# One V product for two groups of heads in an attention and expert kernel on one core

## Chip, cores and metric

The kernel runs on one core of one Trainium2 chip. The metric is the device time of one execution in microseconds; the median of the runs shown is 392.6 us.

## What is computed

For 2048 rows of 256 (8 batches of 256 rows), the reference adds two parts to x:

```
q = layernorm(x); kv = context; seg_id = itok
kv_c = kv @ W_kvc; q_c = q @ W_dq
q_nope, q_rope = q_c @ W_uq, rope(q_c @ W_qr)       # 16 heads
k_nope, k_rope, v from kv_c
scores = (q_nope.k_nope + q_rope.k_rope) * scale, masked to k in [seg_id - 8, seg_id]
x = x + (softmax(scores) @ v) @ W_o
gates: the best two of 8 experts for layernorm(x)
x = x + mean of relu(layernorm(x) @ expert_w + expert_b) over the two
```

No seg_id of the input is above 127, so only the first 128 context rows of each batch matter; a flag worked out from the input picks the path described here.

## The kernel before

Rows are worked in 16 tiles of 128 (two a batch). The weights of the up-projections are folded into the query and output weights first, so that a head works in the 64 latent columns of the context: a head's V is the same 128x64 matrix `v_cur` for all heads of a batch, and its output weight is 64x256. The 16 heads of a tile are four groups of four, so there are 64 groups. `walk` runs slots: slot i = 8 b + k starts group i and carries on the groups before it. Each engine has its own `slot` function, and the order of the calls in it is the order of the engine's queue; counting semaphores are the only link between engines. Slots up to 15 are written out, 16 to 55 are a loop over batches, the last 8 and 6 more to drain are written out again. g is k modulo 4, t the tile, r is k modulo 2 and picks a buffer.

In slot i TensorE has, in this order (its `slot`): the gate products of tile t-2 where g is 1; four transposes of the queries of group i (L1092); the query product of group i+1 in three passes of 512 columns (`mm3`, L674 to L676), with rope parts and unrotated parts in one bank `B_Q`; the transposes of the probabilities of group i-2 (L1119); the scores of group i (L1135), four heads in float32, each recorded as two matmuls; where g is 0 the transposes of a normalised row tile (L1144), where g is 2 the two small rank products (L1155, L1156); the output products of group i-3; in slots 2 to 8 the latent product (L371) and in slots 1 to 7 the transposes of x (L354) for later batches; the V product of group i-2 (L1205).

The output of a group is two blocks of 128 rows (two heads of 64 each). For groups below `PLAIN` the output product is one float32 matmul per block with `oT` and `wo_all` (L1182); for the others it is three passes, high by high, high by low and low by high (`mm3`, L674 to L676, with `oT_hi`, `oT_lo`, `wo_hi`, `wo_lo`), accumulated in `B_Y` over the four groups of a tile. The V product is two matmuls, one for the even and one for the odd heads of the group. Each has the 64 columns of `v_cur` stationary and 256 columns of `pT` moving, and writes one half of the partitions of bank `B_O`; the two stand on different halves of the array.

ScalarE in slot i copies the transposed queries qT of group i (L1273), does the second pair of heads' exponentials of group i-1 (`exps`, L1230), copies pT of group i-2 (L1280), copies the unrotated query parts of group i+1 (L1292), does the first two exponentials of group i, in early slots casts expert weights (`we_high`, L387), copies V's result out of `B_O` as `oT` or `oT_hi` (L1320), and in slots 12 to 15 casts output weights (`wo_high`, L312).

VectorE in slot i has small steps of the gate (`top_two`), then the low half `oT_lo` of group i-3 (L1572: `B_O` less `oT_hi`), the two rope products of group i+1 (L1587, L1588), the reciprocal of the sums of group i-1 (L1596), the masked scores and maxima of group i (L1625), and at g = 2 the sum x2 of the last tile (L1634) with its statistics, at g = 3 the places of rows and the normalised row (L1682 to L1701).

GpSimd joins the rope parts to the query (L1349, group i+1), normalises the probabilities (L1363, group i-1), takes the root of the second norm (L1369), scatters normalised rows to HBM (L1382), builds masks, and in slots 12 to 15 makes the low halves of the output weights (`wo_low`, L316).

After slot 63 the experts' jobs begin (turn, product and store of 128 gathered rows each), eleven of them between the draining slots, the rest after them, and then the sums are stored.

The fold of the output weights (`fold_o`, L301) has the form of the V product: per pair of heads two matmuls of 64 stationary and 256 moving columns on the two halves of the array; a call has four matmuls for two pairs.

Of the kernel before, what the change touches and what calls it, by code (L numbers as in the profile page):

```python
# [23 lines left out]
F32 = mybir.dt.float32  # L24
F32R = mybir.dt.float32r
# [40 lines left out]
def kernel_program(nc, x, ctx_t, ctx_near, itok, w_kvc, w_dq, w_uq_t, w_qr, w_uk_t, w_kr, w_uv_t, w_o,  # L66
                   gate_w, gate_b, expert_w, expert_b, rope, w_kvc_t, out):
    with ExitStack() as ctx:
# [148 lines left out]
        prec = [sb(f"prec{i}", [P, HG]) for i in range(2)]  # L217
        pT = [sb(f"pT{i}", [P, HG, P]) for i in range(2)]
        oT_hi = [sb(f"oT_hi{i}", [P, 2, P], F32R) for i in range(2)]
        plain_mem = ExitStack()  # L220
        oT = [plain_mem.enter_context(nc.sbuf_tensor(f"oT{i}", [P, 2, P], F32)) for i in range(2)]
        plain_mem.close()
        oT_lo = [sb(f"oT_lo{i}", [P, 2, P], F32R) for i in range(2)]
        m_after, m_before = sb("m_after", [P, P]), sb("m_before", [P, P])
# [170 lines left out]
        FOLDS, EXPERT_PIECES = PAIRS // 2, DC * NE // 2  # L395
        PLAIN = 13

        def plain(n):

            return isinstance(n, int) and n < PLAIN  # L400

        def piece_of(i, count):
# [584 lines left out]
        def _(pe):  # L987
# [60 lines left out]
            def dense(f):  # L1048

                kc, j = f % GPT, dense_turned(f // GPT)  # L1050
                if f == 0:
                    pe.wait_ge(m["oT_lo_done"], GROUPS - PLAIN)
                elif f == 1:
                    pe.wait_ge(m["x2_done"], TILES)
                else:
                    pe.wait_ge(m["relu_done"], f - 1)
                cols = slice(512 * kc, 512 * kc + 512)
                z = DENSE_BANK[f % 2]
                pe.matmul(z, ones2[:], bias2[:, cols], start=True, stop=False)
                for c in range(DC):  # L1060
                    mm = mm3(pe, z, xT_hi[j][:, c, :], xT_lo[j][:, c, :], we_hi[:, c, cols], we_lo[:, c, cols],
                             start=False, stop=(c == DC - 1))
                mm.then_inc(m["e_done"], 1)
# [10 lines left out]
            def slot(b, k):  # L1074
# [90 lines left out]
                if isinstance(i, int) and i == 2:  # L1165
                    fold_o(pe, 3)
                if live(i - 3, GROUPS):

                    gp = (k - 3) % GPT
                    at_least(pe, "oT_done", i - 2)  # L1170
                    if not plain(i - 3):
                        pe.wait_ge(m["oT_lo_done"], i - 2 - PLAIN)
                    if isinstance(i, int) and i - 3 < FOLDS:
                        pe.wait_ge(m["wo_done"], FOLDS)
                    if not isinstance(i, int):
                        pe.wait_ge(m["wo_lo_done"], FOLDS)
                    if gp == 0:
                        at_least(pe, "x2_done", TPB * b + (k - 3) // GPT)
                    for q in range(2):
                        first, last = gp == 0 and q == 0, gp == GPT - 1 and q == 1  # L1180
                        if plain(i - 3):
                            mm = pe.matmul(B_Y[:, 0:D], oT[1 - r][:, q, :], wo_all[:, 2 * gp + q, :],  # L1182
                                           start=first, stop=last)
                        else:
                            mm = mm3(pe, B_Y[:, 0:D], oT_hi[1 - r][:, q, :], oT_lo[1 - r][:, q, :], wo_hi[:, 2 * gp + q, :],
                                     wo_lo[:, 2 * gp + q, :], start=first, stop=last)
                    mm.then_inc(m["y_done"], 1)
# [4 lines left out]
                if piece_of(i - 1, B - 1):  # L1192
                    x_turn(pe, i)
                if live(i - 2, GROUPS):

                    if (k - 2) % SLOTS == 0:
                        at_least(pe, "v_ready", b + (k - 2) // SLOTS + 1)
                    at_least(pe, "pT_sb", i - 1)
                    at_least(pe, "oT_done", i - 2)
                    if not plain(i - 3):  # L1200
                        pe.wait_ge(m["oT_lo_done"], i - 2 - PLAIN)
                    if isinstance(i, int) and i == 2:
                        pe.wait_ge(m["wo_done"], 2)
                    for odd in range(2):
                        mm = pe.matmul(B_O[KVC * odd:KVC * odd + KVC, 0:D], v_cur[:], pT[r][:, odd::2, :],  # L1205
                                       start=True, stop=True)
                    mm.then_inc(m["pv_done"], 1)
# [17 lines left out]
        def _(act):  # L1225
# [41 lines left out]
            def slot(b, k):  # L1267
# [9 lines left out]
                if live(i - 2, GROUPS):  # L1277
                    at_least(act, "pT_done", i - 1)
                    at_least(act, "pv_done", i - 3)
                    act.copy(pT[r][:], B_PT[:, :].rearrange("p (h n) -> p h n", h=HG)).then_inc(m["pT_sb"], 1)  # L1280
                late_turn = isinstance(i, int) and i >= GROUPS
# [32 lines left out]
                if piece_of(i - 7, EXPERT_PIECES):  # L1314
                    we_high(act, i - 7)
                if live(i - 2, GROUPS):
                    at_least(act, "pv_done", i - 1)
                    at_least(act, "y_done", i - 3)
                    cols = oT[r][:] if plain(i - 2) else oT_hi[r][:]
                    act.copy(cols, B_O[:, 0:D].rearrange("p (q n) -> p q n", q=2)).then_inc(m["oT_done"], 1)  # L1320
                if piece_of(i - 12, FOLDS) and i < 2 * SLOTS:
# [108 lines left out]
        def _(dve):  # L1430
# [128 lines left out]
            def slot(b, k):  # L1559
# [7 lines left out]
                if g == 1 and live(t - 2, TILES) and not late:  # L1567
                    top_two("gate_step", t - 2, [1])
                if live(i - 3, GROUPS) and not plain(i - 3):
                    at_least(dve, "oT_done", i - 2)  # L1570
                    at_least(dve, "y_done", i - 4)
                    dve.tensor_tensor(oT_lo[1 - r][:], B_O[:, 0:D].rearrange("p (q n) -> p q n", q=2),  # L1572
                                      oT_hi[1 - r][:].bitcast(F32), ALU.subtract).then_inc(m["oT_lo_done"], 1)
                if isinstance(i, int) and i == 8:
                    dve.wait_ge(S("ld_gate_bias"), 16)
                    dve.wait_ge(S("counted"), 6)
                if live(i + 1, GROUPS):

                    j1 = ((k + 1) // GPT) % 2
                    if isinstance(i, int) and i == -1:  # L1580
# [8 lines left out]
                                      a.rearrange("p h (a n) -> p h a n", a=2)[:, :, ::-1, :], sin,  # L1589
                                      ALU.mult).then_inc(m["rope_parts"], 1)  # L1590
                if piece_of(i - 1, B - 1):
                    x_norm(dve, i)
# [4 lines left out]
                if (k - 2) % SLOTS == 0 and live(bv, B):  # L1597

                    at_least(dve, "pv_done", SLOTS * bv)
                    if isinstance(bv, int) and bv == 0:  # L1600
                        dve.wait_ge(S("kcat_done"), 4)
                    kv = kcat[:, bass.ds(bv, 1), 0:KVC]
                    dve.tensor_copy(v_cur[:], kv.rearrange("p a n -> p (a n)")).then_inc(m["v_ready"], 1)
# [27 lines left out]
                if g == 2 and live(t - 1, TILES):  # L1631

                    at_least(dve, "y_done", GPT * t)
                    dve.tensor_tensor(x2_of(t - 1), B_Y[:, 0:D], x2_of(t - 1), ALU.add).then_inc(m["x2_done"], 1)  # L1634
# [169 lines left out]
```

## Time and profile before

| what | value |
| --- | --- |
| median of 3 runs | 392.6 us (391.34 to 395.19) |
| the profiled execution | 392.47 us |
| its span, first to last instruction | 390.6 us |
| mean granted TensorE clock | 0.979 |
| busy: TensorE matmul, weight load | 353.8 us (91%), 290.2 us (74%) |
| busy: VectorE, ScalarE, GpSimd | 276.5 (71%), 262.5 (67%), 234.0 us (60%) |
| chain that ended last: TensorE, VectorE, issue, GpSimd | 73%, 9%, 7%, 5% |

The profile is of one execution. Times in rows are from the span's start. PE is TensorE, PEld its weight loads, DVE VectorE, ACT ScalarE, POOL GpSimd. Matmuls are pipelined: a row's duration overlaps with the next, so that the cost of a piece on TensorE is read from one start to the next.

### The profile page before, as it was taken

Reading aid. Unit: us, or ns where it says so; the run is one execution under the profiler, and the core shown is the slowest. Engines: PE = TensorE matmul, PEld = TensorE weight load, DVE = VectorE, ACT = ScalarE, POOL = GpSimd, SP = SyncE. Lnnn points to the kernel's source line nnn. Section 1 sums busy time; section 2 is a strip of 40 time slices with the busy share of each in tenths; the row PEclk is TensorE's granted clock in tenths of the full one; section 3 lists DMA queues with packets and bytes.
Section 4 is the critical chain, followed back from the end, with each engine's and each line's share of the span. In section 5 each row is a group of like instructions: output and inputs, shape, how many; then the busy total and the mean of one; then the engine's idle time right before and its main releaser. Section 6 shows DMA issues by size and latency. Waiting matters only on the chain.

```text
span 390.6 us, 10358 instructions
## 1 busy us (share of the span) xinstructions
PE 353.8 (91%) x2507; PEld 290.2 (74%) x2507; DVE 276.5 (71%) x1395; ACT 262.5 (67%) x907; POOL 234.0 (60%) x326
## 2 busy tenths in 40 slices
PE   0979999999999999999999999999999788999940
PEld 0866777776778887888888888888887677888730
DVE  2358789687887878778777777778779566444365
ACT  1327777788877887877878877878788544555430
POOL 4626456367987767768577675776865355455500
PEclk9989999999999999999999999999999999999985
DMA  8955040000000000000000000000000354453178
GB/s 273 345 198 215 3 110 3 1 3 27 2 30 1 30 10 17 27 0 27 0 27 27 0 27 0 27 27 0 30 2 28 97 166 127 146 141 113 34 262 294
DMA packets 15094, 28.27 MB, mean 72 GB/s; under 512 B 2892, under 2 KB 10719, under 8 KB 14416
## 3 DMA queue, kind: packets, MB, share of 16 engines
q1 hardware_dynamic: 11408, 20.25, 16.3%
q0 software_dynamic: 2960, 6.94, 5.0%
q10 hardware_dynamic: 688, 0.64, 0.6%
q8 instruction: 16, 0.26, 0.3%
q14 instruction: 22, 0.18, 0.2%
HBM read 17.81 MB, written 10.91 MB: 74 GB/s over the span
## 4 chain that ended last, share of the span: by engine, by line
PE 73%; DVE 9%; issue 7%; POOL 5%; DMA 2%; ACT 2%; ACTq 0%; DVEq 0%; POOLq 0%
PE psum L1135 12%; PE psum L674 9%; PE psum L675 9%; PE psum L676 9%; PE psum L1205 8%; PE psum L1092 8%; PE psum L1119 6%; DVE x_all L1557 2%; DMA wcat<-in_w_kvc 2%; PE psum L1182 2%; PE psum L371 2%; POOL prob L1363 2%; PE psum L1014 1%; POOL q_sb L1349 1%; PE psum L1026 1%
## 5 line engine op out<-in xcount | busy, mean ns | idle before, releaser
L1230 ACT ACTIVATE prob<-nsc,nmax 128x128 f32<-128x128 f32 x256 | 100.7, 396 | 42.9 <-DVE nmax L1625 42.8
L1349 POOL TENSOR_TENSOR q_sb<-rope_a,rope_b 128x256 f32<-128x256 f32 x64 | 47.6, 743 | 57.6 <-DVE rope_b L1588 53.5
L1625 DVE CUSTOM_DVE_ANT_0 nsc<-psum,mask 128x128 f32<-128x128 f32 x256 | 58.9, 286 | 21.3 <-PE psum L1135 21.3
L1363 POOL TENSOR_TENSOR prob<-prob,prec 128x512 f32<-128x512 f32 x64 | 67.1, 1049 | 7.3 <-DVE prec L1596 7.3
L1135 PE MATMUL psum<-kT_all,qT 128*128 (+1 forms) x512 | 69.0, 278 | 1.1 <-ACT qT L1273 1.1
L1135 PEld LDWEIGHTS psum<-kT_all,qT 128*128 128x128 f32 x512 | 62.9, 193 | 2.4 <-ACT qT L1273 2.0
L1417 POOL DMA_INDIRECT halves<-jout,jidx x33 | 32.2, 977 | 30.2 <-ACT jout L1245 13.4
L1230 ACT ACTIVATION_READ_ACCUMULATOR prob<-nsc,nmax 128x1 f32 x256 | 48.4, 189 | 0.0
L1092 PE MATMUL psum<-ident,q_sb 128*128 128x128 f32 x256 | 42.4, 289 | 1.8 <-POOL q_sb L1349 1.7
L1092 PEld LDWEIGHTS psum<-ident,q_sb 128*128 128x128 f32 x256 | 27.2, 142 | 20.9 <-issue 12.3
L1205 PE MATMUL psum<-pT,v_cur 128*64 128x256 f32 x256 | 41.7, 405 | 0.0
L1273 ACT COPY qT<-psum 128x512 f32<-128x512 f32 x64 | 37.5, 585 | 5.4 <-PE psum L1092 3.2
L1119 PE MATMUL psum<-ident,prob 128*128 128x128 f32 x256 | 38.6, 272 | 0.4 <-POOL prob L1363 0.4
L1119 PEld LDWEIGHTS psum<-ident,prob 128*128 128x128 f32 x256 | 31.6, 140 | 9.6 <-POOL prob L1363 0.9
L1382 POOL DMA_INDIRECT slots<-row,place_i x26 | 26.9, 1036 | 16.2 <-POOL row L1377 11.2
L1280 ACT COPY pT<-psum 128x512 f32<-128x512 f32 x64 | 36.5, 571 | 0.1
L674 PE MATMUL psum<-wo_hi,oT_hi 128*128 128x256 f32 x102 | 32.9, 322 | 2.2 <-issue 1.2
L1587 DVE TENSOR_TENSOR rope_a<-psum,ropeq 128x256 f32<-128x256 f32 x64 | 26.7, 416 | 7.7 <-PE psum L676 7.6
L674 PE MATMUL psum<-wq_hi,qc_hi 96*128 96x512 f32 x64 | 30.7, 480 | 0.0
L1292 ACT COPY q_sb<-psum 128x256 f32<-128x256 f32 x64 | 24.2, 377 | 6.9 <-DVE rope_b L1588 6.8
L675 PE MATMUL psum<-wo_lo,oT_hi 128*128 128x256 f32 x102 | 28.5, 279 | 0.0
L676 PE MATMUL psum<-wo_hi,oT_lo 128*128 128x256 f32 x102 | 28.3, 278 | 0.0
(204 smaller groups left out, 864.7 us busy)
## 6 DMA issues: line engine op xcount, KB each, us to landing
wanted<-slots SPq DMA_DIRECT2D x33, 129.0 KB, 2.4
wo_raw<-in_w_o SPq DMA_DIRECT2D x2, 1024.0 KB, 15.5
we_raw<-in_expert_w SPq DMA_DIRECT2D x1, 2048.0 KB, 9.0
half<-halves SPq DMA_DIRECT2D x4, 512.0 KB, 7.3
x_all<-in_x SPq DMA_DIRECT2D x2, 640.0 KB, 17.9
slots<-pad_row SPq DMA_DIRECT2D x8, 129.0 KB, 3.4
we_raw<-in_ctx_near SPq DMA_DIRECT2D x1, 1024.0 KB, 12.0
out<-x_all SPq DMA_DIRECT2D x2, 512.0 KB, 4.7
```

Of the source, the lines that this page charges most:

```text
L674: pe.matmul(out_ap, l_hi, r_hi, start=start, stop=False)
L675: pe.matmul(out_ap, l_hi, r_lo, start=False, stop=False)
L676: return pe.matmul(out_ap, l_lo, r_hi, start=False, stop=stop)
L1092: mm = pe.transpose(B_QT[:, P * h:P * h + P], q_sb[r][:, h, :], ident[:])
L1119: mm = pe.transpose(B_PT[:, P * h:P * h + P], prob[r][:, h, :], ident[:])
L1135: mm = pe.matmul(B_S[r][:, h, :], qT[r][:, h, :], batch_keys, start=True, stop=True)
L1205: mm = pe.matmul(B_O[KVC * odd:KVC * odd + KVC, 0:D], v_cur[:], pT[r][:, odd::2, :], start=True, stop=True)
L1230: e = act.activation(prob[r][:, h, :], nsc[r][:, h, :], ACT.Exp, bias=nmax[r][:, h:h + 1], scale=-1.0, accum_out=psum_h[r][:, h:h + 1])
L1273: act.copy(qT[r][:], B_QT[:, :].rearrange("p (h n) -> p h n", h=HG)).then_inc(m["qT_sb"], 1)
L1349: pool.tensor_tensor(q_sb[1 - r][:, :, KVC:P], rope_a[1 - r][:], rope_b[1 - r][:], ALU.add).then_inc(m["rope_joined"], 1)
L1363: pool.tensor_tensor(p[:], p[:], prec[1 - r][:, :].unsqueeze(2).to_broadcast([P, HG, P]), ALU.mult).then_inc(m["prob_normed"], 1)
L1625: e = dve.tensor_tensor_reduce(nsc[r][:, h, :], B_S[r][:, h, :], mask[(k // GPT) % 2][:], -SCALE, BIG, ALU.add, ALU.min, nmax[r][:, h:h + 1])
```

## The change

The V product is made in odd slots alone, for the two groups before, with 512 moving columns in each half; the output products of both groups are made in the next (even) slot. `pT`, `oT`, `oT_hi` and `oT_lo` hold two groups and are single buffers. ScalarE copies the whole bank `B_O` once, at the end of the odd slot; VectorE makes the low half of all of it once, in the even slot, and there behind the rope products instead of ahead of them. `PLAIN` goes from 13 to 12. Counts on `pv_done`, `y_done`, `oT_done` and `oT_lo_done` are pairs instead of groups.

```diff
-        pT = [sb(f"pT{i}", [P, HG, P]) for i in range(2)]
-        oT_hi = [sb(f"oT_hi{i}", [P, 2, P], F32R) for i in range(2)]
+        pT = sb("pT", [P, 2 * HG, P])
+        oT_hi = sb("oT_hi", [P, 4, P], F32R)
...
-        PLAIN = 13
+        PLAIN = 12
...
+        def pair_of(b, k):
+
+            return (SLOTS // 2) * b + k // 2
...
-                if live(i - 3, GROUPS):
-
-                    gp = (k - 3) % GPT
-                    at_least(pe, "oT_done", i - 2)
-                    if not plain(i - 3):
-                        pe.wait_ge(m["oT_lo_done"], i - 2 - PLAIN)
...
+                if k % 2 == 0 and live(i - 4, GROUPS):
+
+                    gp, p = (k - 4) % GPT, pair_of(b, k - 4)
+                    at_least(pe, "oT_done", p + 1)
+                    if not plain(i - 4):
+                        pe.wait_ge(m["oT_lo_done"], p + 1 - PLAIN // 2)
...
-                    for q in range(2):
-                        first, last = gp == 0 and q == 0, gp == GPT - 1 and q == 1
...
+                    for q in range(4):
+                        first, last = gp == 0 and q == 0, gp == GPT - 2 and q == 3
...
-                if live(i - 2, GROUPS):
-
-                    if (k - 2) % SLOTS == 0:
-                        at_least(pe, "v_ready", b + (k - 2) // SLOTS + 1)
+                if k % 2 == 1 and live(i - 3, GROUPS):
+
+                    p = pair_of(b, k - 3)
+                    if (k - 3) % SLOTS == 0:
+                        at_least(pe, "v_ready", b + (k - 3) // SLOTS + 1)
                     at_least(pe, "pT_sb", i - 1)
-                    at_least(pe, "oT_done", i - 2)
+                    at_least(pe, "oT_done", p)
...
                     for odd in range(2):
-                        mm = pe.matmul(B_O[KVC * odd:KVC * odd + KVC, 0:D], v_cur[:], pT[r][:, odd::2, :],
-                                       start=True, stop=True)
+                        mm = pe.matmul(B_O[KVC * odd:KVC * odd + KVC, :], v_cur[:], pT[:, odd::2, :], start=True, stop=True)
...
-                    at_least(act, "pv_done", i - 3)
-                    act.copy(pT[r][:], B_PT[:, :].rearrange("p (h n) -> p h n", h=HG)).then_inc(m["pT_sb"], 1)
+                    at_least(act, "pv_done", pair_of(b, k - 2))
+                    act.copy(pT[:, HG * r:HG * r + HG, :], B_PT[:, :].rearrange("p (h n) -> p h n", h=HG)).then_inc(m["pT_sb"], 1)
...
-                if live(i - 2, GROUPS):
-                    at_least(act, "pv_done", i - 1)
-                    at_least(act, "y_done", i - 3)
-                    cols = oT[r][:] if plain(i - 2) else oT_hi[r][:]
-                    act.copy(cols, B_O[:, 0:D].rearrange("p (q n) -> p q n", q=2)).then_inc(m["oT_done"], 1)
+                if k % 2 == 1 and live(i - 3, GROUPS):
+                    p = pair_of(b, k - 3)
+                    at_least(act, "pv_done", p + 1)
+                    at_least(act, "y_done", p)
+                    cols = oT[:] if plain(i - 3) else oT_hi[:]
+                    act.copy(cols, B_O.rearrange("p (q n) -> p q n", q=4)).then_inc(m["oT_done"], 1)
...
-                if live(i - 3, GROUPS) and not plain(i - 3):
-                    at_least(dve, "oT_done", i - 2)
-                    at_least(dve, "y_done", i - 4)
-                    dve.tensor_tensor(oT_lo[1 - r][:], B_O[:, 0:D].rearrange("p (q n) -> p q n", q=2),
-                                      oT_hi[1 - r][:].bitcast(F32), ALU.subtract).then_inc(m["oT_lo_done"], 1)
...
                                       a.rearrange("p h (a n) -> p h a n", a=2)[:, :, ::-1, :], sin,
                                       ALU.mult).then_inc(m["rope_parts"], 1)
+                if k % 2 == 0 and live(i - 4, GROUPS) and not plain(i - 4):
+                    p = pair_of(b, k - 4)
+                    at_least(dve, "oT_done", p + 1)
+                    at_least(dve, "y_done", p)
+                    dve.tensor_tensor(oT_lo[:], B_O.rearrange("p (q n) -> p q n", q=4), oT_hi[:].bitcast(F32),
+                                      ALU.subtract).then_inc(m["oT_lo_done"], 1)
```

## Rows read from the trace of the kernel before

**Rows 1.** Busy time by stretch, columns PE, PEld, DVE, ACT, POOL, clock, DMA, GB/s.

```profile
240.00:280.00 40.00, 40.00 (x306) 33.19 (x304) 31.31 (x182) 31.90 (x120) 28.63 (x39) 1.00 0.06 20
```

**Rows 2.** The chain that ended last, slots 53 and 54: start, us, what.

```profile
262.60 0.58 PE psum L1205 x4
263.18 0.59 PE psum L1092 x4
```

**Rows 3.** Timeline of TensorE, slots 53, 54 and 56: start, us, operation.

```profile
260.83 1.06 PE L1135 MATMUL psum<-kT_all,qT 128*128 x8
261.65 0.37 PE L674 MATMUL psum<-wo_hi,oT_hi 128*128 128x256 f32 x1
261.85 0.28 PE L675 MATMUL psum<-wo_lo,oT_hi 128*128 128x256 f32 x1
...
262.53 0.65 PE L1205 MATMUL psum<-pT,v_cur 128*64 128x256 f32 x4
263.11 0.66 PE L1092 MATMUL psum<-ident,q_sb 128*128 128x128 f32 x4
...
264.73 1.06 PE L1135 MATMUL psum<-kT_all,qT 128*128 x8
...
265.68 0.36 PE L674 MATMUL psum<-wo_hi,oT_hi 128*128 128x256 f32 x1
...
273.70 0.36 PE L674 MATMUL psum<-wo_hi,oT_hi 128*128 128x256 f32 x1
```

**Rows 4.** Timeline of ScalarE, slots 53 and 54.

```profile
261.23 0.56 ACT L1280 COPY pT<-psum 128x512 f32<-128x512 f32 x1
...
262.66 0.40 ACT L1230 ACTIVATE prob<-nsc,nmax 128x128 f32<-128x128 f32 x1 [0.60 <-DVE nmax L1625]
...
263.45 0.35 ACT L1320 CAST oT_hi<-psum 128x256 fp32r<-128x256 f32 x1
263.80 0.59 ACT L1273 COPY qT<-psum 128x512 f32<-128x512 f32 x1
```

**Rows 5.** Timeline of VectorE, slots 53, 54 and 56.

```profile
262.12 0.29 DVE L1625 CUSTOM_DVE_ANT_0 nsc<-psum,mask 128x128 f32<-128x128 f32 x1 [0.58 <-PE psum L1135]
...
264.23 0.42 DVE L1572 TENSOR_TENSOR oT_lo<-psum,oT_hi 128x256 fp32r<-128x256 f32 x1
264.58 0.41 DVE L1587 TENSOR_TENSOR rope_a<-psum,ropeq 128x256 f32<-128x256 f32 x1
264.91 0.41 DVE L1588 TENSOR_TENSOR rope_b<-psum,ropeq 128x256 f32<-128x256 f32 x1
...
272.28 0.41 DVE L1572 TENSOR_TENSOR oT_lo<-psum,oT_hi 128x256 fp32r<-128x256 f32 x1
```

**Rows 6.** Timeline of GpSimd, slot 53.

```profile
262.19 0.75 POOL L1349 TENSOR_TENSOR q_sb<-rope_a,rope_b 128x256 f32<-128x256 f32 x1
```

**Rows 7.** Groups by line, whole span: form, count, busy us, mean ns, idle before.

```profile
L1273 ACT COPY qT<-psum 128x512 f32<-128x512 f32 x64 | 37.5, 585 | 5.4 <-PE psum L1092 3.2
...
L392 DVE TENSOR_TENSOR we_lo<-we_raw,we_hi 128x512 fp32r<-128x512 f32 x8 | 7.0, 878 | 0.0
...
L421 DVE TENSOR_TENSOR wq_lo<-psum,wq_hi 96x512 fp32r<-96x512 f32 x2 | 1.4, 678 | 0.0
```

**Rows 8.** The chain that ended last, slot 2, a fold of output weights.

```profile
38.05 1.01 PE psum L301 x8
```

**Rows 9.** Timeline of ScalarE and TensorE, slots 5, 9 and 10.

```profile
54.19 0.38 ACT L1292 COPY q_sb<-psum 128x256 f32<-128x256 f32 x1
...
78.05 0.61 ACT L387 CAST we_hi<-we_raw 128x512 fp32r<-128x512 f32 x1
...
79.51 1.11 PE L1135 MATMUL psum<-kT_all,qT 128*128 128x128 f32 x8
```

**Rows 10.** Timeline of TensorE and VectorE near 321 us.

```profile
321.89 0.44 PE L1144 MATMUL psum<-ident,row 128*128 128x128 f32 x2 [0.99 <-DVE row L1701]
...
321.36 0.47 DVE L1701 TENSOR_SCALAR row<-x_all,mv,rstd 128x256 f32<-128x256 f32 x1 [1.75 <-POOL rstd L1369]
```

## What I predict before seeing the changed kernel

> **What bounds the kernel now.** I read the busy time by stretch first. From 240 to 280 us TensorE is busy for every microsecond, at the full clock, while VectorE and ScalarE stand near 80% and GpSimd near 70% [rows 1]. Then the chain of waits: through the slots it is TensorE alone, products end to end [rows 2]. The starts on TensorE's timeline give one slot its prices [rows 3]: from the transposes of the queries (L1092, 263.11) to the scores (L1135, 264.73) 1.62; scores to the output product (L674, 260.83 to 261.65) 0.82; output products to the V product (261.65 to 262.53) 0.88, of which the first takes 0.20, the other five about 0.117 each (0.585), and the rest, 0.09, is a gap ahead of V; V to the next transposes (262.53 to 263.11) 0.58. Sum 3.90. A slot with the rank products costs 0.13 more (264.73 to 265.68 is 0.95 against 0.82); what the other kinds of slot add is the same before and after.
>
> But TensorE is not alone at the limit. ScalarE's timeline [rows 4] has, after the scores: exponentials at 262.66, the output copy at 263.45, the query copy (qT) at 263.80 to 264.39, and the next scores at 264.73. ScalarE waited 0.60 before the exponentials and almost nowhere after: the loop scores, maxima, exponentials, output copy, query copy, next scores has about 0.3 us of slack.
>
> **The change part by part.** Slots now alternate. An odd slot has no output products and one V product over both groups; an even slot has twelve output products and no V.
>
> V, on TensorE. Two products cost 2 x (0.09 + 0.58) = 1.34 a pair of slots. The new one, 512 columns a half, is not in the trace. Lower bound: nothing more for the doubled columns, 0.58. Upper: the halves no longer run beside each other, two of today's for each half, about 1.7. The nearest row is the folding of the weights (L301), the same form with two halves of 64 columns and twice 256 columns in a row: 1.01 for eight records [rows 8]. I take 1.01, with 0.09 ahead of it: a gain of 0.24 a pair. Output products: two first ones at 0.20 become one, a gain of 0.08. Together 0.32 of TensorE's time a pair.
> The trace shows the cost of the switch between V's half-width form and full-width work: transposes after V hold the chain for 0.59 [rows 2]. The Trainium skill (TensorEngine Tiling (Array Packing), Key Properties) says that a change of tiling mode drains TensorE; by that rule half the drains go, and the sum would be the full 0.32 a pair, which is the first rival below.
>
> The path through ScalarE in an odd slot. I lay the odd slot on the times of rows 3 to 5. Scores start 260.83; the first maximum runs at 262.12 and the exponentials at 262.66 [rows 4, 5], as before: nothing in between changes. The output copy starts at 263.45; V, now at 261.65 + 0.09, has ended by 263, so it does not hold it (the copy of pT ends at 261.79 [rows 4] and may hold V's start by 0.1, under this cover). The copy is now 128x512 instead of 128x256: the nearest rows are the query copy, 128x512 from PSUM, 585 ns [rows 7], against 350 ns. Successive operations overlap by about 0.10, so the query copy starts at 263.45 + 0.48 = 263.93 and ends at 264.52; with 0.05 for the wait the even slot's scores start at 264.57. TensorE by itself would be there at 260.83 + 0.82 + 0.09 + 1.01 + 1.62 = 264.37. So it stands 0.20, and, since the weights of the first score product are no longer loaded under other work, about 0.08 more. Of the 0.32, 0.28 is gone. In the even slot ScalarE has no output copy and is early; its time cannot be given back there, since TensorE sets that slot.
> The Trainium skill (TensorEngine Tiling (Array Packing), PSUM Bottleneck) warns that faster tiled products do not speed up the emptying of PSUM, which may become the bound; the trace agrees so far as its ScalarE loop has only 0.3 us of slack.
>
> VectorE in the even slot. The low half (L1572) is now 128x512 and stands behind the two rope products. At 256 columns it took 0.42 [rows 5]; at 512 the nearest rows are 678 ns (L421, 96x512 from PSUM) and, as the upper end, 878 ns (L392) [rows 7]; the lower end is the old 0.42. I take 0.69. In the slot of the rank products the ropes move from 264.58 to 264.23, the low half starts two steps of 0.33 later, 264.89, and ends at 265.58, 265.63 with the wait. TensorE wants it at 264.57 + 0.82 + 0.08 + 0.13 = 265.60. In the other even slot VectorE comes free at 272.28 [rows 5]: 272.28 + 0.66 + 0.69 + 0.05 = 273.68, against TensorE, whose first output product stood at 273.70 [rows 3] and by the same steps comes 0.08 earlier, 273.62. So the low half costs 0.03 to 0.07 a pair. What waits behind it on VectorE is the reciprocal and the maxima; GpSimd's normalisation of the odd group then starts about 0.3 later, which is in time for its transposes a slot later. The rope joins (L1349) come 0.3 earlier except behind the scatter issues, where GpSimd starts the join at 262.19 and ends it at 262.94 whatever VectorE does [rows 6]: 0.2 after TensorE's new 262.75, hidden under the stand of 0.20 above.
> Sum for the 24 pairs of slots 16 to 63: 0.32 - 0.28 - 0.06 is about -0.02 a pair, a loss of 0.5 us in all, which is nothing within its error.
>
> The slots before 16. Pairs 3 to 8 carry the latent product, which waits for the copy of the unrotated queries (L1292, to 54.57 [rows 9]). Odd slots reach it at 54.30 instead of a product later: a stand of 0.3. The odd slot then ends at 57.10 (before 57.15), and the even one, with 0.87 more of plain output products and without V and its gap (0.67), takes 0.20 more: 0.17 a pair lost, 0.5 in three. In pairs 9 to 12 ScalarE also casts expert weights (L387, 78.05, step 0.51) between the exponentials and the output copy [rows 9]: copy at 78.56, query copy 79.05 to 79.63, scores at 79.68 instead of 79.51, and 0.20 + 0.08 in the even slot: 0.45 a pair, 0.9 in two. Slots 13 to 16 wait for GpSimd's low halves of the output weights, before and after: 0. Group 12 becoming split (PLAIN 12) falls there too: 0.
>
> The end. The last pair's V now comes whole in slot 65. The copy behind it is 0.22 longer, the low half 0.27, the products 0.70: 1.19 more on the way to the last tile's sum. TensorE does about 0.37 less in slot 65 and is there earlier: 0.8 net. That way is on the path: TensorE stood 0.99 us for that row (L1144 at 321.89), and VectorE 1.75 for its root [rows 10].
>
> The single buffers of pT and oT cost nothing: the slots between their uses are filled by the work above, and the halved counts change no order on a DMA queue.
>
> Sum: 0.5 + 0.5 + 0.9 + 0.8 = 2.7 us (the loop, pairs 3 to 8, pairs 9 to 12, the end). The profiled execution took 392.47 (span 390.6, 1.9 around it, unchanged): 395.2. The median of the runs shown is 392.6, so the profile stands for them.
>
> **The rivals.** First, TensorE stays the bound: 0.32 x 24 = 7.7 us gained, less 0.8 at the end: 385.6. For it: TensorE is the whole chain of waits. Against it: the ScalarE loop in rows 4, unless the wide copy takes nearer 0.35 than 0.585. Second, slower: VectorE's low half decides. At 0.88 instead of 0.69 every even slot stands 0.19 longer: 24 x 0.19 = 4.6 us, 399.8. It decides once the low half takes more than about 0.66, at the place where TensorE waits ahead of the twelve products. For it: VectorE runs without a pause from the maxima to that point. Against it: L421 is the nearer row, as it reads PSUM. Third, the change doesn't do what it says: V's halves of 512 columns run one behind the other, 0.7 more per odd slot; 0.5 of that shows after the stand of 0.20: 12 us, 407. The L301 row speaks against it. Fourth, the stand is half what I find: 24 x 0.14 = 3.4 us better, 391.8.
>
> **How the numbers follow.** The forecast, 395.2 with its own range from 392 to 398, gets 0.5; TensorE-bound 0.15; the half stand 0.15; VectorE's low half 0.17; V's halves apart 0.03. About 1% (3.9 us) is what a measurement of this kernel tells from no change: faster is below 388.7, slower above 396.5. Faster: 0.15, and 0.02 of the half stand's lower edge, 0.17. Slower: 0.17 + 0.03 + 0.13 of the forecast's upper part, 0.33. The rest, 0.50, is within 1%. The range for 8 in 10 goes from 387.5 to 400: it leaves out most of the first rival and the third.
>
> **What would show it.** Right: TensorE idle 0.1 to 0.3 before the scores of even slots, released by the query copy; that copy starting 0.48 after an output copy of 0.58; the low half ending within 0.1 of the first output product; V at about 1.0 from its start to the transposes; pairs of slots near the 7.93 (3.90 and 4.03) that they take now. Wrong: pairs of 7.6 (first rival), output products waiting over 0.2 for the low half (second), V near 1.7 (third).

## The result, and the profile after

The changed kernel takes 400.78 us (median of 4 runs, 399.68 to 401.42) against 393.36 (391.34 to 395.19) for the kernel before, run beside it: 1.0187 times as long [1.0127, 1.0247]. I had said 395.2, at most 400. The profiled execution took 401.42 (span 399.7). The starts of the query transposes divide the 9.1 us between the spans: slot 17 starts 1.07 later than before (110.84 and 111.91), slot 61 5.78 (292.04 and 297.82), slot 63 6.77 (300.54 and 307.31), and from there to the end it is 92.35 instead of 90.07.

Of the first 1.07, 0.40 stands already at slot 1 (29.17 and 29.57), ahead of all that the change moves (the kernel of b4_turns_late, which is the kernel before up to slot 63, is there at 28.55); slot 2, where V no longer stands, is 0.69 shorter (6.65 and 5.96), which I had not priced; from slot 3 to slot 17 the loss is 1.36 (69.79 and 71.15), where I had 1.4. The end lost 2.28 instead of 0.8, and the slots from 17 to 62 lost 5.7 instead of 0.5: slots 17 to 60 4.71, of which the pairs with g = 1 and 2 have 0.97 and those with g = 3 and 0 3.74, and slots 61 and 62 0.99.

The share of the chain of waits by engine, from the profile's page, shows what kind of loss it is. TensorE had 73%, and has 55% now:

```profile
PE 55%; DVE 16%; issue 12%; POOL 7%; ACT 5%; DMA 2%; DVEq 1%; ACTq 0%; SPq 0%; POOLq 0%
```

First the parts that I had priced. The chain in slots 53 and 54 (start, us, what) has V at 1.01 for both groups, as in [rows 8], with the transposes at 0.59 behind it, as in [rows 2]:

```profile
267.05 1.01 PE psum L1209 x4
268.05 0.59 PE psum L1096 x4
```

ScalarE's timeline in the same slots, beside [rows 4]: the wide output copy takes 0.56, and the query copy starts 0.47 behind its start (I had 0.48):

```profile
268.60 0.56 ACT L1324 CAST oT_hi<-psum 128x512 fp32r<-128x512 f32 x1
269.07 0.58 ACT L1276 COPY qT<-psum 128x512 f32<-128x512 f32 x1
```

TensorE's timeline, slots 54 (g = 2) and 56 (g = 0), beside [rows 3]:

```profile
267.99 0.66 PE L1096 MATMUL psum<-ident,q_sb 128*128 128x128 f32 x4
268.40 0.48 PE L678 MATMUL psum<-wq_hi,qc_hi 96*128 96x512 f32 x1
...
268.95 0.39 PE L680 MATMUL psum<-wq_hi,qc_lo 96*128 96x512 f32 x1
...
269.78 1.15 PE L1139 MATMUL psum<-kT_all,qT 128*128 x8
...
270.88 0.39 PE L678 MATMUL psum<-wo_hi,oT_hi 128*128 128x256 f32 x1
...
272.40 0.60 PE L1096 MATMUL psum<-ident,q_sb 128*128 128x128 f32 x4
272.75 0.47 PE L678 MATMUL psum<-wq_hi,qc_hi 96*128 96x512 f32 x1
...
275.96 0.66 PE L1096 MATMUL psum<-ident,q_sb 128*128 128x128 f32 x4
...
277.68 1.16 PE L1139 MATMUL psum<-kT_all,qT 128*128 128x128 f32 x8
278.67 0.38 PE L1148 MATMUL psum<-ident,row 128*128 128x128 f32 x2
279.32 0.36 PE L678 MATMUL psum<-wo_hi,oT_hi 128*128 128x256 f32 x1 [0.27 <-issue]
```

and before, the starts of slots 55 and 56 and the scores of slot 56:

```profile
267.14 0.66 PE L1092 MATMUL psum<-ident,q_sb 128*128 128x128 f32 x4
...
271.04 0.66 PE L1092 MATMUL psum<-ident,q_sb 128*128 128x128 f32 x4
...
272.67 1.06 PE L1135 MATMUL psum<-kT_all,qT 128*128 128x128 f32 x8
```

In slot 54 the scores come 1.79 behind the transposes instead of 1.62 (I had 0.20 to 0.28 more) and the slot takes 4.41. With the odd slot's 3.62 the pair takes 8.03; I had about 7.95, before it was 7.93. That pair is nearly right. The pair with g = 3 and 0 is not: 3.56 and 5.23 instead of 3.90 and 4.58. In slot 56 the first output product comes 1.64 behind the scores; before it was 273.70 - 272.67 = 1.03, and I had 0.06 more.

VectorE's timeline says why, after:

```profile
269.47 0.42 DVE L1586 TENSOR_TENSOR rope_a<-psum,ropeq 128x256 f32<-128x256 f32 x1
...
270.14 0.68 DVE L1594 TENSOR_TENSOR oT_lo<-psum,oT_hi 128x512 fp32r<-128x512 f32 x1
...
272.71 0.42 DVE L1639 TENSOR_TENSOR x_all<-psum,x_all 128x256 f32 x1 [0.62 <-PE psum L680]
...
274.29 0.42 DVE L1586 TENSOR_TENSOR rope_a<-psum,ropeq 128x256 f32<-128x256 f32 x1
...
277.52 0.44 DVE L1706 TENSOR_SCALAR row<-x_all,mv,rstd 128x256 f32 x1 [0.37 <-POOL rstd L1373]
277.89 0.41 DVE L1586 TENSOR_TENSOR rope_a<-psum,ropeq 128x256 f32<-128x256 f32 x1
...
278.55 0.67 DVE L1594 TENSOR_TENSOR oT_lo<-psum,oT_hi 128x512 fp32r<-128x512 f32 x1
```

and before, in the same slots (the low half and the ropes of slot 56 are in [rows 5]):

```profile
266.86 0.42 DVE L1634 TENSOR_TENSOR x_all<-psum,x_all 128x256 f32 x1
...
268.68 0.42 DVE L1587 TENSOR_TENSOR rope_a<-psum,ropeq 128x256 f32<-128x256 f32 x1
```

Read each against the start of its slot. The sum x2 of the last tile ran 0.28 ahead of slot 55 (which began at 267.14), without a wait. Now it runs 0.31 behind the start (272.40), and has waited 0.62 for the output products. Before, V stood between those products and the next slot, and the sum had that time; now the twelve products are the last work of the slot. Its statistics follow on VectorE, and the ropes of slot 55 start 1.89 behind its start instead of 1.54. From there it goes through GpSimd, whose queue has the rope join, the normalisation and only then the root. GpSimd after and before:

```profile
275.13 0.73 POOL L1353 TENSOR_TENSOR q_sb<-rope_a,rope_b 128x256 f32<-128x256 f32 x1 [2.27 <-DVE rope_b L1587]
275.82 1.04 POOL L1367 TENSOR_TENSOR prob<-prob,prec 128x512 f32<-128x512 f32 x1
276.81 0.57 POOL L1373 TENSOR_TENSOR rstd<-veps,half_neg 128x1 f32<-128x1 f32 x1
```

```profile
269.51 0.73 POOL L1349 TENSOR_TENSOR q_sb<-rope_a,rope_b 128x256 f32<-128x256 f32 x1 [1.56 <-DVE rope_b L1588]
270.20 1.04 POOL L1363 TENSOR_TENSOR prob<-prob,prec 128x512 f32<-128x512 f32 x1
271.20 0.57 POOL L1369 TENSOR_TENSOR rstd<-veps,half_neg 128x1 f32<-128x1 f32 x1
```

The root starts 0.85 into slot 56 instead of 0.16. VectorE waits 0.37 for it ahead of the row (L1706), which starts 1.56 into the slot instead of 0.86; the rest of that delay is VectorE's own, from the late sum. Behind the row stand the ropes and then the low half: this ends 3.26 into the slot (279.22), where I had 2.59, and TensorE's output products start 0.10 behind it. The table of waits (us in total, times, longest) shows the same links over the whole span; before, the row waited 3.3 us in all for the root, and TensorE 0.5 for low halves:

```profile
DVE x_all L1639 <- PE psum L680: 8.9, 13, 1.3
...
DVE row L1706 <- POOL rstd L1373: 6.9, 14, 1.8
...
PEld psum L678 <- DVE oT_lo L1594: 4.9, 11, 0.7
...
PE psum L678 <- DVE oT_lo L1594: 3.9, 9, 1.5
```

### The profile page after: what moved, and what is told of

Same layout as the page of the kernel before. It is cut to its first block, busy times and chain, and to the rows that moved or that the text cites. A ratio compares the mean times of both kernels' runs of the same rounds, so it can differ in the third digit from the quotient of the medians.

```text
span 399.7 us, 9958 instructions
## 1 busy us (share of the span) xinstructions
PE 356.3 (89%) x2381; PEld 288.4 (72%) x2381; DVE 281.0 (70%) x1370; ACT 259.9 (65%) x875; POOL 233.5 (58%) x326
## 4 chain that ended last, share of the span: by engine, by line
PE 55%; DVE 16%; issue 12%; POOL 7%; ACT 5%; DMA 2%; DVEq 1%; ACTq 0%; SPq 0%; POOLq 0%
PE psum L678 9%; PE psum L1139 8%; PE psum L680 8%; PE psum L679 8%; PE psum L1096 4%; PE psum L1209 4%; PE psum L1123 3%; POOL prob L1367 3%; DVE x_all L1561 2%; ACT prob L1233 2%; DVE rope_b L1587 2%; DVE oT_lo L1594 2%; PE psum L1186 2%; DMA wcat<-in_w_kvc 2%; PE psum L371 2%
## 5 line engine op out<-in xcount | busy, mean ns | idle before, releaser
L1139 PE MATMUL psum<-kT_all,qT 128*128 (+1 forms) x512 | 71.6, 283 | 2.2 <-ACT qT L1276 1.7
L1096 PE MATMUL psum<-ident,q_sb 128*128 128x128 f32 x256 | 41.0, 283 | 3.0 <-POOL q_sb L1353 3.0
L1209 PE MATMUL psum<-pT,v_cur 128*64 128x512 f32 x128 | 34.5, 617 | 0.2
L680 PE MATMUL psum<-wo_hi,oT_lo 128*128 128x256 f32 x104 | 29.9, 287 | 0.0
L679 PE MATMUL psum<-wo_lo,oT_hi 128*128 128x256 f32 x104 | 29.6, 284 | 0.0
```

Source lines behind the costliest of these rows:

```text
L679: pe.matmul(out_ap, l_hi, r_lo, start=False, stop=False)
L680: return pe.matmul(out_ap, l_lo, r_hi, start=False, stop=stop)
L1096: mm = pe.transpose(B_QT[:, P * h:P * h + P], q_sb[r][:, h, :], ident[:])
L1139: mm = pe.matmul(B_S[r][:, h, :], qT[r][:, h, :], batch_keys, start=True, stop=True)
L1209: mm = pe.matmul(B_O[KVC * odd:KVC * odd + KVC, :], v_cur[:], pT[:, odd::2, :], start=True, stop=True)
```

## The experiments

Theory A: the low half comes too late, by that chain (products, x2, statistics, ropes, join, root, row, ropes, low half). Theory B: ScalarE's wide copy ahead of the query copy, which is what I had built the forecast on. The lengths of slots 53 to 56 (from one start of the query transposes to the next) serve for all runs. Ratios are to the kernel before, run beside them: 392.76 us (e1, e3, e4, e5), 392.62 (e2, e6, e7, b2), 391.93 (b3, b4, e8) and 392.55 (e9).

| run | us | ratio | g = 1, 2, 3, 0 |
| --- | --- | --- | --- |
| before | | 1 | 3.90, 4.03, 3.90, 4.58 |
| after | 400.78 | 1.0187 [1.0127, 1.0247] | 3.62, 4.41, 3.56, 5.23 |
| e1_root_first | 396.69 | 1.0107 [1.0049, 1.0164] | 3.62, 4.43, 3.56, 5.01 |
| e3_low_pass_last | 393.57 | 1.0023 [0.9992, 1.0054] | 3.92, 4.09, 3.58, 4.73 |
| e4_copy_after_q | 400.81 | 1.0196 [1.0143, 1.0249] | 3.62, 4.42, 3.56, 5.24 |
| e5_pass_and_copy | 393.81 | 1.0030 [1.0001, 1.0059] | 4.18, 4.08, 3.56, 4.53 |
| e6_scatter_split | 393.16 | 1.0017 [0.9989, 1.0045] | 3.66, 4.08, 3.57, 4.90 |
| e7_split_root | 387.73 | 0.9884 [0.9864, 0.9905] | 3.62, 4.09, 3.56, 4.53 |
| e2_low_first | 401.80 | 1.0251 [1.0230, 1.0271] | 4.52, 4.08, 3.56, 4.72 |
| b3_low_last | 396.17 | 1.0111 [1.0075, 1.0147] | 4.02, 4.03, 4.10, 4.59 |
| b2_split_root | 392.77 | 0.9999 [0.9978, 1.0019] | 3.90, 4.03, 3.90, 4.58 |

**e1_root_first**: on GpSimd the root stands ahead of the join.

```diff
+                if g == 3 and live(t - 1, TILES):
+
+                    at_least(pool, "ln_step", 3 * t)
+                    at_least(pool, "x2n_done", t - 1)
+                    pool.tensor_tensor(rstd2[:], veps2[:], half_neg[:, 0:1], ALU.pow).then_inc(m["rstd2_done"], 1)
                 if live(i + 1, GROUPS):
```

> Changed kernel, with GpSimd's root of the second norm moved ahead of the rope join in the slots with g = 3. Theory A (the loss is the low half that TensorE waits for in the slots with g = 0, and it is late because the tile's sum on VectorE waits for twelve products and pushes ropes, join, normalisation, root, row and ropes behind it): the row on VectorE starts near 1.1 us of the g = 0 slot instead of 1.54, the first output product near 3.0 instead of 3.30, these slots take 4.9 instead of 5.19 (5.15 instead of 5.44 at the start of a loop turn), 12 x 0.3 = 3.6 us off: 397. Theory B (the wide output copy on ScalarE ahead of the query copy is what costs): no change, 400.8.

396.69, as expected: 3.9 us above the kernel before instead of 7.4. One move in the queue of an engine that is busy for 60% of the span gives back half of the loss; of the slots in the table only the one with g = 0 is shorter. The row starts 1.39 into that slot (I expected 1.1) and no longer waits. The link through the root is shown. The first link, the sum that comes late because the products now end the slot, no run takes away by itself: it is read from the rows.

**e3_low_pass_last**: the eight products that don't read the low half go first, and TensorE waits for it only then.

```diff
-                            mm = mm3(pe, B_Y[:, 0:D], oT_hi[:, q, :], oT_lo[:, q, :], wo_hi[:, 2 * gp + q, :],
-                                     wo_lo[:, 2 * gp + q, :], start=first, stop=last)
+                            pe.matmul(B_Y[:, 0:D], oT_hi[:, q, :], wo_hi[:, 2 * gp + q, :], start=first, stop=False)
+                            pe.matmul(B_Y[:, 0:D], oT_hi[:, q, :], wo_lo[:, 2 * gp + q, :], start=False, stop=False)
+                    if not plain(i - 4):
+                        pe.wait_ge(m["oT_lo_done"], p + 1 - PLAIN // 2)
+                        for q in range(4):
+                            mm = pe.matmul(B_Y[:, 0:D], oT_lo[:, q, :], wo_hi[:, 2 * gp + q, :], start=False,
+                                           stop=gp == GPT - 2 and q == 3)
```

> Changed kernel, with the eight output products that don't read the low half first, and the wait for the low half behind them. Theory A: the wait disappears under 0.94 us of products; slots with g = 0 take 4.85 to 5.1 instead of 5.19 and 5.44, slots with g = 2 4.35 to 4.4, and about 1 us less at the end where slot 62 waits for the low half: 395 to 396. Theory B: no change, 400.8.

393.57, better than expected: 0.8 us above the kernel before is left of 7.4, so the wait for the low half carries nearly the whole loss. In the loop it comes back in the slots with g = 0 (4.73 instead of 5.23). The slot with g = 2 is shorter too (4.09), but only because the one before it is longer (3.92): the pair takes 8.01, after the change 8.03. TensorE now waits there for the rope join, and ScalarE has time to be early:

```profile
262.77 0.66 PE L1096 MATMUL psum<-ident,q_sb 128*128 128x128 f32 x4 [0.23 <-POOL q_sb L1356]
```

**e4_copy_after_q**: ScalarE's wide copy goes behind the query copy, into the even slot.

```diff
-                if k % 2 == 1 and live(i - 3, GROUPS):
-                    p = pair_of(b, k - 3)
...
+                if k % 2 == 0 and live(i - 4, GROUPS):
+                    p = pair_of(b, k - 4)
...
                     act.copy(cols, B_O.rearrange("p (q n) -> p q n", q=4)).then_inc(m["oT_done"], 1)
```

> Changed kernel, with ScalarE's wide output copy moved from the end of the odd slot to behind the query copy of the even slot. Theory B: scores of the even slot start 1.62 us into it instead of 1.80 to 1.90, all of 0.28 a pair comes back: 24 x 0.28 = 6.7 us, 394. Theory A: the scores start earlier, but the first output product stands where it stood in the slots with g = 0, held by the low half, and gains at most 0.1 in those with g = 2: 399.5 to 400.8.

No gain, every slot as long as without the edit: taking the wide copy out of the way gives nothing by itself. The scores of slot 54 do come at 1.63 instead of 1.79, but the low half is not earlier, and TensorE waits for that instead (the totals were 4.9 and 3.9 after the change):

```profile
269.79 0.38 PE L678 MATMUL psum<-wo_hi,oT_hi 128*128 128x256 f32 x1 [0.18 <-DVE oT_lo L1594]
```

```profile
PEld psum L678 <- DVE oT_lo L1594: 10.0, 20, 0.9
...
PE psum L678 <- DVE oT_lo L1594: 9.2, 22, 1.7
```

So the two waits stand one behind the other, and this run alone can't say what the copy costs; the next one does.

**e5_pass_and_copy**: both of the last two edits.

> Both edits together: the low pass last, and the wide copy behind the query copy. If the two waits stand behind one another (theory A with B under it), TensorE alone bounds the pairs: 7.6 us for those with g = 2, 8.2 for those with g = 0, 0.3 a pair less than the kernel before: 24 x 0.3 = 7 us less than it, about 387 with the losses of the first and last slots. If theory A alone holds, it is no better than the low pass last alone, 395 to 396; if B alone, no better than the copy alone, 394.

A miss in the total: 393.81, no better than the low pass alone. With the low half out of the way the copy's move is worth 0.20 in the slot with g = 0 (4.53 instead of 4.73), near the 0.28 that I had for the copy; but the next slot gives it back (4.18 instead of 3.92). GpSimd's timeline there has the rope join behind two scatter issues, at 261.31, and TensorE's transposes of slot 54 wait for it. I had found that join 0.2 late and called it hidden under ScalarE's wait; that holds only as long as there is such a wait:

```profile
258.94 1.09 POOL L1389 DMA_INDIRECT slots<-row,place_i  x1 [0.94 <-POOL row L1384]
260.33 0.97 POOL L1389 DMA_INDIRECT slots<-row,place_i  x1 [0.30 <-issue]
261.31 0.75 POOL L1356 TENSOR_TENSOR q_sb<-rope_a,rope_b 128x256 f32<-128x256 f32 x1
```

```profile
262.12 0.66 PE L1096 MATMUL psum<-ident,q_sb 128*128 128x128 f32 x4 [0.49 <-POOL q_sb L1356]
```

**e6_scatter_split**: e5, and on GpSimd at g = 0 the token copy and the first scatter issue stand ahead of the join, the second where both were.

```diff
+                if g == 0 and live(t - 3, TILES) and gathered(t - 3):
...
+                    for high in range(1):
+                        pool.indirect_dma_start(slots.ap(), bass.IndirectOffsetOnAxis(place_i[j][:, high:high + 1], 0),
...
                 if live(i + 1, GROUPS):
...
-                    for high in range(2):
+                    for high in range(1, 2):
                         pool.indirect_dma_start(slots.ap(), bass.IndirectOffsetOnAxis(place_i[j][:, high:high + 1], 0),
```

> Low pass last, wide copy behind the query copy, and GpSimd's two scatter issues of a tile split: the token copy and the first issue ahead of the rope join of the slot with g = 0, the second behind its normalisation as now. Theory C (what those two edits free is given back in the slots with g = 1, 4.18 to 4.42 long, because the rope join for the next transposes is queued on GpSimd behind two scatter issues, 3 us with their waits): the slots with g = 1 take 3.6 to 3.8 instead of 4.18, those with g = 0 up to 4.8 instead of 4.52 as the root still stands behind the normalisation: 0.3 x 12 = 3.5 us less, 390. Rival D (TensorE or ScalarE bounds those slots): no change, 393.8.

Half of it: the slot with g = 1 is 3.66, but the one before it 4.90, as the root is late again ahead of this queue.

**e7_split_root**: e6 with e1's move of the root.

> The same with the root of the second norm ahead of the rope join as well. Theory C: slots of 4.55, 3.6, 4.08 and 3.56, 15.8 per tile instead of 16.34 to 16.5, 12 x 0.6 = 7 us less than the two edits alone: 387, below the kernel before. Rival D: 393.8.

387.73, as expected: 1.2% faster than the kernel before and, with e9_table_first below, the best version. The pairs take 7.71 and 8.09 instead of 7.93 and 8.48, 0.30 less on the mean: nearly the 0.32 a pair that I had worked out for TensorE are there once no queue stands against them.

**b2_split_root** (control): the two moves on GpSimd in the kernel before.

> The kernel before, with the split scatter and the root ahead of the join, as a control. If TensorE alone bounds its slots, nothing changes but slots 13 to 16, which wait for GpSimd: 391 to 393. If GpSimd's order was a hidden bound there too, some us faster.

Nothing: without the merged products the order on GpSimd holds nothing up, so the moves are worth only what these make late.

**e2_low_first**: the changed kernel with the low half ahead of the ropes again, where it stood.

> Changed kernel, with the low half of V ahead of the rope products again. Theory A: in the slots with g = 0 the low half is ready 0.66 us earlier and TensorE gets to the output products 0.3 to 0.5 earlier; but the ropes, the join and the normalisation come 0.68 later, the scatter issues and the next join behind them too, and the transposes of the slot with g = 2 wait up to 0.8: between 3 us faster and 6 us slower, 398 to 406. If the order doesn't matter: 400.8.

401.80. The slots with g = 2 and g = 0 are short again (4.08, 4.72); the ropes are late instead, and the join falls behind the scatter issues (4.52). With x2 late, neither place on VectorE is free.

**b3_low_last**: the other half of the change alone, the narrow low half behind the ropes.

```diff
-                if live(i - 3, GROUPS) and not plain(i - 3):
-                    at_least(dve, "oT_done", i - 2)
...
                                       ALU.mult).then_inc(m["rope_parts"], 1)
+                if live(i - 3, GROUPS) and not plain(i - 3):
+                    at_least(dve, "oT_done", i - 2)
```

> One part of the change alone: the kernel before, with its low half (128x256, every slot) moved behind the two rope products. In the kernel before the low half ran from 272.28 in the slot where g is 0, and TensorE's output products stood there at 273.70; behind the ropes it ends 0.66 later, 273.3, still ahead of TensorE. So the theory that the order hurts only together with the merged products (whose sum x2 comes late and whose low half is 0.27 longer) expects no change: 392.2 to 393.2 us, slots of 3.90, 4.03, 3.90, 4.58. The rival, that the order alone costs VectorE's loop time in each slot, expects over 395.

A miss, and one that tells of an input that I had left out: 396.17, the odd slots 53 and 55 0.12 and 0.20 longer, the even ones as before. VectorE and TensorE in slot 57:

```profile
278.99 0.42 DVE L1582 TENSOR_TENSOR rope_a<-psum,ropeq 128x256 f32<-128x256 f32 x1 [0.31 <-PE psum L676]
...
279.67 0.41 DVE L1589 TENSOR_TENSOR oT_lo<-psum,oT_hi 128x256 fp32r<-128x256 f32 x1
```

```profile
278.56 0.40 PE L676 MATMUL psum<-wq_hi,qc_lo 96*128 96x512 f32 x1
...
279.23 1.06 PE L1135 MATMUL psum<-kT_all,qT 128*128 128x128 f32 x8
280.23 0.36 PE L674 MATMUL psum<-wo_hi,oT_hi 128*128 128x256 f32 x1
```

The ropes read the query product of this very slot and can't start before it ends, here at 278.96, after 0.31 of waiting. The low half used to run in that wait. Behind the ropes it ends at 280.08, and the output products start 1.00 behind the scores instead of 0.82. So in the kernel before the order alone costs 4.2 us, in the loop by its odd slots. The changed kernel has no low half there, so this is no part of its loss.

**The end.** In the changed kernel TensorE's clock fell behind slot 63. Stretches of its profile, then of e9_table_first, in which it did not (us, busy of PE, PEld, DVE, ACT, POOL, then the granted clock):

```profile
312.20:314.70 2.50, 1.38 (x8) 0.91 (x9) 1.47 (x5) 2.40 (x10) 1.00 (x2) 0.87 0.51 122
314.70:317.50 2.80, 2.80 (x15) 2.80 (x14) 1.18 (x5) 0.37 (x1) 0.49 (x1) 0.50 0.44 126
```

```profile
300.80:303.70 2.90, 2.02 (x18) 2.05 (x19) 2.03 (x8) 1.77 (x7) 1.04 (x1) 1.00 0.41 114
```

In 314.70 to 317.50 the granted clock is 0.50, the 1.2 GHz level, after a stretch in which TensorE was busy for 1.38 of 2.50 us, and the twelve products of slot 64 run there. Three runs went after what the end lost.

**b4_turns_late** and **e8_turns_late**: the first turns of the jobs, which wait for fetched rows, go behind the output products of slot 64; in the kernel before, and in e7_split_root.

```diff
-                if isinstance(i, int) and i == GROUPS:
-                    first_turns()
                 if isinstance(i, int) and i > GROUPS and g == 1 and live(t - 2, TILES):
...
+                if isinstance(i, int) and i == GROUPS:
+                    first_turns()
                 if piece_of(i - 2, B - 1):
```

> Control for the next: the kernel before, with the turns of the first two jobs (which wait for rows fetched from HBM) moved behind the output products of slot 64. Before, TensorE waited 0.47 us there with six products behind it, and it kept its full clock. Both theories expect a gain of 0 to 0.4: 392.2 to 393.0.

> The fastest version so far (387.73 us) with the same move: the turns of the first two jobs behind the twelve output products of slot 64. Theory: the loss of 2.3 us at the end comes from these twelve products, which stand in TensorE's queue behind a wait of 0.86 and 0.30 us for the fetched rows and then run at the lower clock (0.21 us each instead of 0.12, about 1.0 us in all); moved ahead they start about 1.6 us earlier, and 1.0 to 1.8 us come back: 386.0 to 386.8, slot 63 to end about 91.0. Rival, as the prediction put it: the end is longer because the last pair's V, copy, low half and products come whole in the last slots (1.19 on the way to the last sum); then the move gives nothing beyond what the control gains: 387.3 to 387.7.

Both missed, in the same direction: 393.85, 1.0039 [1.0021, 1.0057], and 389.32, 0.9920 [0.9891, 0.9949]. With the turns later the time from slot 63 to the end grows from 90.07 to 92.36 and from 92.44 to 93.65. So the turns must not come later; whether earlier products alone would give anything these two runs can't tell.

**e9_table_first**: e7_split_root with VectorE's job table ahead of the sum x2 in slot 62.

```diff
+                if isinstance(i, int) and i == GPT * NS + 10:
+                    rows_of_jobs()
                 if g == 2 and live(t - 1, TILES):
...
-                if isinstance(i, int) and GPT * NS + 8 <= i < GPT * NS + 11:
+                if isinstance(i, int) and GPT * NS + 8 <= i < GPT * NS + 10:
```

> The fastest version so far (387.73 us) with VectorE's table of the jobs' rows, in slot 62, ahead of the last tile but one's sum x2 instead of behind it (that sum waits for the twelve products). The last two runs showed that the jobs' first turns may not be delayed: 1.4 us later on TensorE cost 2 us at the end. Theory: what the end lost (slot 63 to end 92.44 against 90.07) began here: the sum comes later, so does the table behind it, the fetch of the rows and the first turns (0.8 later behind the start of slot 63). With the table 1.46 us earlier the first turns stand directly behind the transposes, about 0.9 earlier, and 0.9 to 1.5 come back: 386.2 to 386.9, slot 63 to end 91.0 to 91.6. Rival: the end is set by the last pair's V, copy, low half and products, and the turns only must not be later than they are: 387.4 to 388.2, end about 92.4 or, as the row of the last tile but one is later now, more.

In the profiled execution the end is 91.04, as the theory had it, and the products of slot 64 have the full clock. But the median is 387.83, 0.9883 [0.9863, 0.9903], the same as without the move. The two profiled executions also differ by 0.88 at the start of slot 63, of which 0.86 was there at slot 1 (28.40 and 29.26). From slot 63 to the end the versions with no edit meant for it take between 90.86 (e6_scatter_split) and 92.93 (e4_copy_after_q). So what the end of the changed kernel costs, and how much of it the job table or the clock, stays open.

## Why the prediction was wrong, by its own steps

- **V at 1.01, the wide copy at 0.585, the low half at 0.69**: right (1.01, 0.56, 0.68 from the rows above).
- **Scores of even slots 0.20 to 0.28 late**: right. They come 0.17 late in slot 54 and take 1.15 instead of 1.06, 0.26 together. But this is not what decided: the low half stands behind it, so that e4_copy_after_q gained nothing, and only with the low half out of the way (e5_pass_and_copy) does the copy's move show.
- **"The ropes move from 264.58 to 264.23", the low half ends at 265.58**: right in the slots with g = 2. From the slot's start at 262.75 that is 1.48 and 2.83; in slot 54 it is 1.48 (269.47) and 2.83 (270.82), and TensorE's first output product follows 0.06 later. One input was left out: the ropes read the query product of the same slot, whose last pass before was this one, to 264.45:

```profile
264.06 0.39 PE L676 MATMUL psum<-wq_hi,qc_lo 96*128 96x512 f32 x1
```

  In the changed kernel it ends at 269.34, 0.13 ahead of the ropes, and does not hold them. In b3_low_last it does.
- **"VectorE comes free at 272.28"** in the slots with g = 0: the step that failed. I took VectorE's arrival from before, though the change itself moves it: the output products become the last work of their slot, x2 waits for them, and the delay comes back on VectorE and, as a late root, through GpSimd's queue. The low half ended 3.26 into the slot instead of 2.59. I had 0.03 to 0.07 a pair for it; the pairs with g = 3 and 0 lost 0.34 each, 3.74 of the 4.71 us of slots 17 to 60. e1_root_first shows the part of the root (5.23 to 5.01), e3_low_pass_last that of the whole wait (4.73).
- **Slots before 16**: 1.36 from slot 3 on against 1.4, and 0.69 gained in slot 2 that I had not looked for. **The end**: 2.28 against 0.8; open, as said.
- **The 0.59 of the transposes behind V, read as the cost of a switch**: from their start to the query product's it is 0.41 behind V (267.99 to 268.40) and 0.35 behind the products (272.40 to 272.75). So by starts only 0.06 of it comes from what stands ahead.
- **The rivals**: the second had the right place (TensorE waiting ahead of the twelve products), and its time, 399.8, was within 1 us by luck: I let the low half take 0.88 in every even slot, and it took 0.68 and came late in those with g = 0. The first, TensorE alone, 385.6, is what the kernel comes near to (387.73) with e7_split_root's four moves on TensorE, ScalarE and GpSimd.

## What to carry to other kernels

When work is merged, ask not only what the merged instruction costs but who reads the last result of the group and when it now comes: here a sum that had run under V's time found the products at the very end of the slot. Follow each moved operation to its own inputs as well as to its neighbours in the queue: in b3_low_last the low half had stood ahead of the ropes in a time in which these were waiting anyway. An edit that gives nothing alone may only uncover the next wait (e4_copy_after_q and then e5_pass_and_copy). And an engine at 60% can hold the path by the order of its queue alone; two moves there turned a loss of 0.3% (e5_pass_and_copy) into a gain of 1.2%.

## What the runs showed of the hardware

VectorE's cast qc_hi, 96x128 within SBUF, takes 0.22 us in the kernel before:

```profile
259.23 0.22 DVE L1653 CAST qc_hi<-qc_all 96x128 fp32r x1
```

In e6_scatter_split it took 1.40, beside GpSimd's work:

```profile
257.92 1.40 DVE L1668 CAST qc_hi<-qc_all 96x128 fp32r x1
```

```profile
257.51 0.74 POOL L1371 TENSOR_TENSOR q_sb<-rope_a,rope_b 128x256 f32<-128x256 f32 x1
258.19 1.05 POOL L1385 TENSOR_TENSOR prob<-prob,prec 128x512 f32<-128x512 f32 x1
```

It starts under the join and ends at 259.32, just behind the normalisation (259.24). In e7_split_root it took 0.80 and ended at 254.37, again 0.1 behind a normalisation. The Trainium skill (SBUF — State Buffer, Who interferes with whom) says that VectorE's copies and casts can need a pair of ports that they share with GpSimd, that the engine which issues first has the pair for its whole instruction, and that the other then waits. Both traces agree in where the cast ends; that in e6_scatter_split it did not get in between the join and the normalisation is not explained by that. So a move in one queue can go with a slower neighbour that shares no data with it.
